# Stacked columns of the score stage: transposed by VectorE in 32x32 blocks and by way of DRAM instead of by TensorE

## What is computed

```
query = x @ Wq ; keyt = enc @ Wk ; valt = enc @ Wv
hs = mha(query, keyt, valt)                       # 124 keys
ca_q1 = einsum('btc,th->bch', ca, Wq_ca)[:, indices]   # 2048 rows picked from 384
ca_hs1 = mha(ca_q1, x, x)                         # x itself is key and value
ca_hs2 = mha(ca_hs1 @ Wq, ca @ Wk_ca, ca @ Wv_ca) # 4 keys
out = (hs + ca_hs2) @ Wout + b_out + x
```

## Time and profile before

| | |
|---|---|
| median of three executions | 744.38 us |
| the profiled execution: its time / its span | 744.62 / 742.9 us |
| TensorE matmuls | 714.7 us busy, 96% of the span |
| VectorE | 565.9 us, 76% |
| ScalarE | 375.4 us, 51% |
| GpSimd | 172.2 us, 23% |
| mean granted TensorE clock | 0.998 |
| score stage of batch 0 / batch 1 | about 53.9 to 202 / 398.9 to 544 us |

### The profile page before, as it was taken

One profiled execution on the slowest core, in us unless ns is written; L12 is line 12 of the kernel. 1 busy time (PEld: TensorE's weight loads), 2 busy tenths in 40 slices (PEclk: granted clock), 3 DMA queues, 4 the chain that ended last, 5 costly groups with the idle time before them and its releaser, 6 DMA issues.

```text
span 742.9 us, 12225 instructions
## 1 busy us (share of the span) xinstructions
PE 714.7 (96%) x4507; PEld 654.2 (88%) x4507; DVE 565.9 (76%) x952; ACT 375.4 (51%) x942; POOL 172.2 (23%) x205
## 2 busy tenths in 40 slices
PE   7999999999989999998999999999989998999998
PEld 5978999999867778998999999999967777999997
DVE  3456888888899999676854888888899999665652
ACT  1634444555499993234333555545479996232321
POOL 8033961111200000542230511111110000323120
PEclk9999999999999999999999999999999999999999
DMA  8524353443220008799925344443230005598831
GB/s 275 158 86 113 88 130 89 95 95 101 93 87 2 1 2 158 188 215 208 242 93 112 84 98 95 96 94 93 93 133 2 0 1 114 88 238 201 175 125 68
DMA packets 226852, 82.22 MB, mean 111 GB/s; under 512 B 208284, under 2 KB 210204, under 8 KB 226792
## 3 DMA queue, kind: packets, MB, share of 16 engines
q1 hardware_dynamic: 226792, 81.43, 44.4%
HBM read 50.00 MB, written 31.33 MB: 109 GB/s over the span
## 4 chain that ended last, share of the span: by engine, by line
PE 68%; DVE 11%; issue 6%; SPq 5%; ACT 4%; POOL 3%; DMA 2%; DVEq 0%; ACTq 0%
PE PS L1261 28%; PE PS L1468 15%; PE PS L1447 6%; PE PS L1236 5%; DVE e_lo L1016 4%; SPq L437 3%; PE PS L1363 3%; ACT e_hi L735 3%; PE PS L1208 2%; DVE e_hi L1008 2%; PE PS L1333 2%; PE PS L1173 2%; PE PS L1354 1%; POOL wo_lo L615 1%; POOL wo_hi L610 1%
## 5 line engine op out<-in xcount | busy, mean ns | idle before, releaser
L1261 PE MATMUL PS<-mm_hi,xT_hi 128*128 128x280 f32 (+3 forms) x480 | 159.6, 333 | 0.0
L913 DVE TENSOR_REDUCE mpart<-PS 128x4 f32<-128x512 f32 x192 | 131.5, 686 | 36.8 <-PE PS L1236 36.4
L1261 PE MATMUL PS<-mm_hi,xT_lo 128*128 128x280 f32 (+3 forms) x480 | 157.4, 328 | 0.0
L1261 PE MATMUL PS<-mm_lo,xT_hi 128*128 128x280 f32 (+3 forms) x480 | 156.5, 326 | 0.0
L624 POOL TENSOR_TENSOR xin<-xin,bias 128x640 f32<-128x640 f32 x32 | 50.9, 1594 | 307.1 <-issue 192.5
L576 POOL TENSOR_TENSOR ex<-ex,rinv 128x992 f32<-128x992 f32 x30 | 55.4, 1845 | 201.6 <-DVE rinv L907 201.5
L685 ACT ACTIVATE ex<-PS,neg 128x124 f32<-128x124 f32 x256 | 89.9, 364 | 11.8 <-DVE gs L895 6.5
L1261 PEld LDWEIGHTS PS<-mm_hi,xT_hi 128*128 128x128 f32 x480 | 90.2, 188 | 0.7 <-issue 0.5
L1261 PEld LDWEIGHTS PS<-mm_lo,xT_hi 128*128 128x128 f32 x480 | 90.4, 188 | 0.3
L1261 PEld LDWEIGHTS PS<-mm_hi,xT_lo 128*128 128x128 f32 x480 | 90.3, 188 | 0.2
L777 ACT ACTIVATE oT_hi<-PS 128x256 fp32r<-128x256 f32 x80 | 29.9, 386 | 116.7 <-PE PS L1447 110.0
(11 more groups left out here) (156 smaller groups left out, 1326.7 us busy)
## 6 DMA issues: line engine op xcount, KB each, us to landing
ex_kept<-ex SPq DMA_DIRECT2D x32, 512.0 KB, 2.9
ex<-ex_kept SPq DMA_DIRECT2D x112, 128.0 KB, 3.2
xin<-in_x SPq DMA_DIRECT2D x128, 80.0 KB, 2.9
xin<-in_x SPq DMA_DIRECT2D x32, 320.0 KB, 3.9
out<-res SPq DMA_DIRECT2D x32, 320.0 KB, 3.1
raw_kept<-raw SPq DMA_DIRECT2D x5, 512.0 KB, 2.6
ex<-ex_kept SPq DMA_DIRECT2D x4, 512.0 KB, 4.1
mm_lo<-raw_kept SPq DMA_DIRECT2D x10, 186.0 KB, 2.9
```

The source lines that it names most:

```text
L913: nc.vector.tensor_reduce(mpart[:, n // 2, :, 2 * (n % 2):2 * (n % 2) + 2, i].rearrange("p s k -> p k s"), PS[:, 6 + N % 2, :].rearrange(" ...
L1261: last = mul(PS[:, slot(T, k), p0:p0 + w], l[:, i % 2, j, :], rr[:, m0:m0 + w], start=(j == 0 and n == 0), stop=(n == 2), skip_group_check ...
```

## The change

For tiles 0 to 11 of each batch (`MOVED = 12`) the turning of `gs` leaves TensorE. VectorE transposes `gs` in 32x32 blocks into one buffer `gsT` (`gs_blocks`), SP writes it to a DRAM tensor `g_kept` in four DMAs and reads it back in four DMAs straight into `gT`. In SP's turn for i the four writes of tile i - 1 come first (after a wait for `gs_blocks`), then the four loads of x as before, then the wait for the writes and the four reads, then the wait for the normalisation and the store of ex. The block transpose of a tile waits until the writes of the tile before have landed. TensorE's `g_stack` and ScalarE's copy stay for tiles 12 to 15.

All units move to one tile later: in step i at positions 3, 12, 21 the last three of tile i - 2, and at 35, 39, 43 the first three of tile i - 1. Step 0 has none, step 1 three. Steps 12 and 13 have eight each (positions 3, 8, 13, 23, 28, 33, 38, 43), so that tile 11's first unit is at position 23 of step 12, and the last two steps begin with five units (2, 7, 12, 17, 22) instead of three. From step 12 on the backlog is made good; the end of the stage is as before.

```diff
+MOVED = 12
+        gsT = sb("gsT", [P, NH * SLOTS])
+        def stacked(T):
+            return T // TILES * (TILES - MOVED) + max(T % TILES - MOVED, 0)
+        def moved(T):
+            return T // TILES * MOVED + min(T % TILES, MOVED)
+        def uses(T):
+            return T // TILES * MOVED // 2 + T % TILES // 2
+        def units_of(i):
+            first = (0, 0, 3) + tuple(9 + 6 * n for n in range(10)) + (71, 79, 87)
+            return [(q // UNITS, q % UNITS) for q in range(first[i], first[i + 1])]
+        g_kept = nc.dram_tensor("g_kept", (B, MOVED, SLOTS, NH, P), F32, kind="Internal").ap()
...
 @block.sync
+                def move_in(i):
+                    sp.wait_ge(g_out[i % 2], (uses(b * TILES + i) + 1) * 64)
+                    if b and i == 0:
+                        sp.wait_ge(sT_ps, b * QUADS)
+                    rows = g_kept[b, i].rearrange("k (s r) n -> r k s n", s=SETS)
+                    for r in range(R):
+                        sp.dma_start(gT[r * SLOTS:(r + 1) * SLOTS, :, i * P:(i + 1) * P].bitcast(F32), rows[r]).then_inc(g_in[i % 2], 16)
                     if i >= 1:
+                        if i - 1 < MOVED:
+                            sp.wait_ge(gsT_made, moved(T - 1) + 1)
+                            for n in range(P // SLOTS):
+                                sp.dma_start(g_kept[b, i - 1, :, :, n * SLOTS:(n + 1) * SLOTS],
+                                             gsT[n * SLOTS:(n + 1) * SLOTS, :].rearrange("k (h t) -> k h t", h=NH)).then_inc(g_out[(i - 1) % 2], 16)
                         sp.wait_ge(xTr_made, T)
                         load_x(x_use(b, 0, i - 1) + X_BUFS)
+                        if i - 1 < MOVED:
+                            move_in(i - 1)
                         sp.wait_ge(norm_made, T)
...
 @block.scalar
-                    g(i)
+                    if i >= MOVED:
+                        g(i)
...
 @block.vector
+                def gs_blocks(i):
+                    T = b * TILES + i
+                    dve.wait_ge(gs_made, T + 1)
+                    if moved(T):
+                        dve.wait_ge(g_out[(i - 1) % 2], ((moved(T) - 1) // 2 + 1) * 64)
+                    nc.vector.transpose(gsT[:, :], gs[:, i % 2].rearrange("p h n -> p (h n)")).then_inc(gsT_made, 1)
...
                 for i in range(1, TILES - 1):
+                    units = units_of(i)
+                    more = len(units) > UNITS
+                    a, c = (0, 0) if len(units) < UNITS else (1 + more, 4 if more else 3)
                     least(i - 1, 2)
-                    unit(i - 1, HERE)
+                    for q in units[:a]:
+                        unit(*q)
...
                     g(i)
-                    unit(i - 1, HERE + 1)
+                    for q in units[a:a + 1] if a else ():
+                        unit(*q)
+                    if i < MOVED:
+                        gs_blocks(i)
                     xT(i + 1)
                     y_low(i - 1, 2)
-                    unit(i - 1, HERE + 2)
+                    for q in units[a + 1:c] if a else ():
+                        unit(*q)
                     inv(i - 1)
                     least(i, 1)
-                    for n in range(HERE):
-                        unit(i, n)
+                    for q in units[c:]:
+                        unit(*q)
...
 @block.tensor
                 def unit(i, n):
-                    if n == 0:
-                        pe.wait_ge(gT_made, b * TILES + i + 1)
+                    if n == 0 and i < MOVED:
+                        pe.wait_ge(g_in[i % 2], (uses(T) + 1) * R * 16)
+                    elif n == 0:
+                        pe.wait_ge(gT_made, stacked(T) + 1)
...
-                UNIT_AT = {3: (-1, 3), 12: (-1, 4), 21: (-1, 5), 35: (0, 0), 39: (0, 1), 43: (0, 2)}
+                UNIT_AT = (3, 12, 21, 35, 39, 43)
+                MORE_AT = (3, 8, 13, 23, 28, 33, 38, 43)
...
                 def step(i):
+                    units = units_of(i)
+                    units_at = dict(zip(MORE_AT if len(units) > UNITS else UNIT_AT[-len(units):], units)) if units else {}
                     for k in range(3):
-                        scores(i, k, 15 * k, {q: (i + d, n) for q, (d, n) in UNIT_AT.items() if i + d >= 0}, {26: i})
+                        scores(i, k, 15 * k, units_at, {26: i} if i >= MOVED else {})
```

More of the change, by code:

```diff
@@ L343, in build @@
         gsh_made, gs_made, gT_ps, gT_made = sem("gsh_made"), sem("gs_made"), sem("gT_ps"), sem("gT_made")
+        gsT_made, g_out, g_in = sem("gsT_made"), [sem("g_out0"), sem("g_out1")], [sem("g_in0"), sem("g_in1")]
         rinv_made, norm_made = sem("rinv_made"), sem("norm_made")
@@ L697, in g @@
                     T = b * TILES + i
-                    act.wait_ge(gT_ps, T + 1)
+                    act.wait_ge(gT_ps, stacked(T) + 1)
                     nc.scalar.activation(gT[:, :, i * P:(i + 1) * P], PS[:, 5, P:P + SETS * P].rearrange("p (s n) -> p s n", s=SETS),
@@ L706, in _ @@
                 exps(0, 0)
-                g(0)
                 if b:
@@ L890, in g @@
                     T = b * TILES + i
-                    if T >= 2:
-                        dve.wait_ge(gT_ps, T - 1)
+                    if T >= 2 and (T - 2) % TILES < MOVED:
+                        dve.wait_ge(gsT_made, moved(T - 2) + 1)
+                    elif T >= 2:
+                        dve.wait_ge(gT_ps, stacked(T - 2) + 1)
                     nc.vector.tensor_copy(gs_half(i, 0).bitcast(F32R), g_rep(T)).then_inc(gsh_made, 1)
@@ L930, in _ @@
                 xT(1)
+                gs_blocks(0)
                 least(0, 1)
-                for n in range(HERE):
-                    unit(0, n)
                 if b == 0:
@@ L1214, in g_stack @@
                     T = b * TILES + i
-                    if T:
-                        pe.wait_ge(gT_made, T)
+                    if stacked(T):
+                        pe.wait_ge(gT_made, stacked(T))
                     pe.wait_ge(gs_made, T + 1)
@@ L1238, in unit @@
                     last.then_inc(mx_ps, 1)
-                UNIT_AT = {3: (-1, 3), 12: (-1, 4), 21: (-1, 5), 35: (0, 0), 39: (0, 1), 43: (0, 2)}
-                LAST_AT = {3: (-2, 3), 12: (-2, 4), 21: (-2, 5), 33: (-1, 0), 37: (-1, 1), 41: (-1, 2), 45: (-1, 3), 49: (-1, 4), 53: (-1, 5),
+                UNIT_AT = (3, 12, 21, 35, 39, 43)
+                MORE_AT = (3, 8, 13, 23, 28, 33, 38, 43)
+                LAST_AT = {2: (-2, 1), 7: (-2, 2), 12: (-2, 3), 17: (-2, 4), 22: (-2, 5), 33: (-1, 0), 37: (-1, 1), 41: (-1, 2), 45: (-1, 3), 49: (-1, 4), 53: (-1, 5),
                            58: (0, 0), 62: (0, 1), 66: (0, 2), 70: (0, 3), 74: (0, 4), 78: (0, 5)}
@@ L1305, in _ @@
                 last_steps()
-                pe.wait_ge(gT_made, (b + 1) * TILES)
+                pe.wait_ge(gT_made, (b + 1) * (TILES - MOVED))
                 pe.wait_ge(asm_made, b + 1)
```

## The result

| | kernel before | changed kernel |
|---|---|---|
| median (lowest to highest) | 745.0 us (742.5 to 746.4) | **795.0 us** (787.7 to 802.9) |
| profiled execution, time / span | 744.62 / 742.9 us | 787.71 / 786.0 us |
| mean granted TensorE clock, profiled | 0.998 | 0.989 |
| score stage (first to last score matmul), batch 0 / batch 1 | 147.7 / 144.6 us | 172.7 / 162.2 us |

The ratio is **1.0655** (95% interval 1.062 to 1.069); it leaves out the execution of 802.9 us, the one with the lowest granted clock (0.965). Slower was forecast, at 753 us and with 770 as the upper end: the direction held, the size did not. All of the difference lies in the score stage: 25.0 us in batch 0, 17.6 in batch 1, 42.6 of the 43.1 that the span grew.

What follows compares the result with a forecast made beforehand. TensorE bounds the score stage before; after the change the latency of SP's column DMAs takes over its pace. Batch 0 +5.9 us and batch 1 +2.8 us, +8.7 on 744.62, give 753 us; range 746 to 770.

Steps and rivals of the forecast that it cites:

- The path through SP sets the pace: Score stage: TensorE waits for columns moved by SP's in-order queue; a step takes 9.14 us, so the saving is gone.
- Rival A: Short DMA latency, L 7.2, steady steps at 8.83 us: +2.5 us, 747 us, no change; chance 0.17.
- C: Rival: VectorE's block transpose waits for the previous tile's writes; at a 6 us landing +20, 765 us; chance 0.08.
- B: Rival: columns always in SBUF when asked for, all hidden; 5.3 us come back, 739 us; chance 0.13.
- The recurrence: S = t(m) + 10.28 us, t(m+2) = t(m) + 10.28 + L; t: first unit behind a step's 36th matmul.
- L: Latency from S to the last landed read of a tile's columns: 8.0 us, bounds 7.2 and 11.2.
- S: Start of SP's store of ex after its normalisation wait; 92.0 and 102.0 us for tiles 2 and 3, batch 0.
- four writes: SP's writes of a tile's columns to DRAM, 256 runs of 128 bytes: 0.45 us each, 1.8 (1.5 to 3.0).
- three reads ahead of the last: SP's issue of reads back from DRAM, 64 runs of 512 bytes: 0.34 us each, 1.0 (0.9 to 2.1).
- store and gap: First term of L: SP's store of ex and the gap to its next issue, 0.38 us.
- landing: Last term of L: the last column read's landing after its issue, taken as 2.0 us.
- Steps of 8.83 us: Score-stage step without DMA wait: 9.05 us less 0.22 us of TensorE for the removed pair of transposes.

Runs made afterwards that it cites:

- experiment 3: Kernel before with only the units moved one tile later; all tiles still turned on TensorE, no block transposes or column DMAs: 744.9 us, ratio 1.001.
- experiment 4: Changed kernel with all additions but nothing removed: reads land in an unused place, used columns still come from TensorE and ScalarE: 749.0 us, ratio 1.0077.
- experiment 1: Changed kernel with SP's queue reordered: column writes as soon as VectorE has them, ahead of the store of ex; reads behind it: 760.8 us, ratio 1.023.
- experiment 5: Changed kernel with SP's order turned round (early writes) and the columns read back in one DMA, behind the store of ex: 741.0 us, ratio 0.9968.
- experiment 7: Changed kernel with early writes and one read, the read also ahead of SP's wait for the normalisation and store of ex: 737.3 us, ratio 0.9939.
- experiment 8: Changed kernel plus ten unused 128x256 matmuls ahead of each TensorE wait for the columns: 778.1 us, ratio 1.048 to the kernel before.
- experiment 2: Changed kernel with the DRAM copy laid out head by head, so one DMA reads it back instead of four; SP's order unchanged: 762.1 us, 1.0245.
- experiment 9: The changed kernel, unchanged, measured again on the same chip beside the run with filler matmuls: 790.1 us, ratio 1.0643 to the kernel before.

## Why the prediction was wrong

**The path through SP sets the pace: right.** Experiments 3 and 4 show that the shift costs nothing measurable and all that is added, without the wait for it, 5 us (749.0 against 743.8); 1 and 5 show that the place in the queue costs the most. Rival A (no change) is out, and so is C: the block transposes waited 1.3 us in all. B, all hidden, fell for the kernel as it stands and came true in experiment 7, with the writes earlier, one read instead of four, and both ahead of SP's wait.

**The recurrence: right.** t(m) + 10.28 was measured as 10.37 to 10.39 in most turns at full clock, and as 11.9 to 12.1 in three where the clock fell behind the unit (one: unit at 146.35, store at 158.26). With the measured L = 10.2 its own working gives +16.3 us for batch 0 and +16.0 for batch 1, 774 us beside the 742.0 of the last group, beyond the range too; with the clock held up, experiment 8 measured 778.1. No run separates what is left.

**A wait that was left out: step 2 of batch 0.** I let the stores of tiles 2 and 3 hang on GpSimd alone and put TensorE's first wait into step 4. But the store of tile 0 came at 72.21 and the columns of tile 1 landed 9.7 us later, and TensorE stood still for 3.44 us. GpSimd then waited 1.6 us for VectorE's reciprocal of tile 2, and S came at 94.06, not 92.0. My own terms had this wait: the unit stood at 80.14 before, 1.82 us are taken away ahead of it, which gives 78.3, and with L = 8.0 the columns land at 80.2.

**The step that failed: the size of "four writes" and "three reads ahead of the last".** I put 0.45 and 0.34 us an issue, "by the number of runs". Measured: 0.65 both, so 2.6 and 1.96 instead of 1.8 and 1.0, together 1.8 of the 2.2 us. In the means over the 22 turns, beside my terms: store and gap 0.41 (0.38), writes 2.67 (1.8), loads of x 2.95 (2.85), reads 2.05 (1.0), landing 2.12 (2.0); the means lie above the medians because single issues took up to 1.9 us. The trace before had warned: the loads of x (640 runs, median 0.65) and block loads of ex (1024 runs, median 0.69, a line that I did not show) cost nearly the same per issue, so the number of runs was not what sets it. Experiment 2, where the same runs in another order took 0.455 us, says so too, and no row had these shapes. The upper bound 0.70 was the better value to build on. At 10.2 us, L was inside my bounds (7.2 to 11.2), but the range ended at L = 9.6.

**What was missing altogether: the clock.** I took TensorE at full clock, as the earlier trace rows have it. In the changed kernel it falls to 1.2 GHz, half, behind most of the long pauses. Two stretches of the profiled execution, the first behind the pause of 2.91 us shown above, the second ahead of it, and last the first stretch's times in the kernel before (columns as under experiment 8):

```profile
147.00:150.20 3.20, 3.20 (x13) 3.16 (x12) 1.28 (x2) 0.00 (x0) 0.00 (x0) 0.50 0.49 91
...
136.80:146.00 9.20, 6.64 (x43) 6.27 (x42) 6.41 (x15) 4.12 (x19) 1.84 (x1) 1.00 0.45 92
...
147.00:150.20 3.20, 3.20 (x25) 3.18 (x24) 3.17 (x9) 2.03 (x8) 0.00 (x0) 1.00 0.72 136
```

There are 13 matmuls in 3.2 us, where the kernel before has 25. Four such stretches, of 3.4 us each, lie in batch 0, behind pauses of 3.44, 2.91, 3.41 and 4.31 us. But a pause of 2.90 us (ahead of the unit at 104.31) had none, nor had those of 2.5 to 3.0 us in batch 1, while in experiments 2, 4, 5 and 9 stretches at half clock go with pauses of 2.0 to 2.9 us. Outside this stage some stand behind pauses of 0.6 to 1.1 us, one of them in the kernel before (at 631 us, behind 0.56 and 0.76). So the pauses go with the fall, but their length alone does not decide it.

Experiments 8 and 9 price it: 12 us in the median. It goes with the spread too: the six executions of experiment 9 run from 785.4 us at clock 0.985 to 794.5 at 0.974; a span times what its clock lacks of 1 is 11.8 us in the one and 20.6 in the other, about as far apart as the times. So of the 48 us by which the changed kernel was slower there, 36 are waits and 12 the clock that the waits bring down.

**The rule of the Trainium skill** ("DMA: Bandwidth & Descriptors", Specifications: under 512 bytes read-modify-write). The 128-byte writes landed 1.9 us after their issue at the least and 2.1 in the median; in the turn shown, the last landed at S + 4.3, 1.4 us before SP came to the reads, and over the whole run SP waited for them once, 0.4 us. By the rule the reads would have been moved; here its effect, if there is one, was covered, and no run compares the writes with longer ones.

**Steps of 8.83 us: right.** Experiment 7 has them in all of steps 2 to 11, experiment 5 in all but two, so the pair of transposes was worth 0.22 us, not the 0.54 of two durations.

## What to carry to other kernels

Work moved from a busy engine to DMAs is paid in issue time of one queue and in the order of that queue: write down the queue's whole turn, its waits for unrelated work too, and compare both its length and the path from the last unrelated wait to the landing with the step of the engine that sets the pace. Issue a transfer where its data is ready, ahead of waits for other data. Price an unseen DMA's issue by the dearest row of a like shape, and price repeated pauses of TensorE of some 2 to 4 us with the clock that may follow.

## What the runs showed of the hardware that I had not expected

- An issue by SP took 0.59 to 0.61 us in the median for 32 KB over 32 partitions, whether 256 runs of 128 bytes or 64 of 512, and 0.65 from one to the next; 128 KB read over 128 partitions in one DMA took 0.38 to 0.68 (experiments 2 and 5). With the axes of the DRAM tensor in another order the same 256 runs took 0.455 (experiment 2).
- TensorE's clock was 1.2 GHz around or behind pauses of 2.0 to 5.2 us, for 3.4 or 6.8 us each time, though not at every such pause; matmuls without use in the pauses prevented all of it in the score stage (mean clock of the profiled executions 0.974 without, 0.998 with them).
- Moving the columns' DMAs to GpSimd's queue went with one operation of VectorE of 7.2 us, where the median is 0.78, while GpSimd worked for 6.1 us; the cause is open.
